# Routed experts computed only for their tokens, instead of every expert for every token

## The chip, the cores and the metric

The kernel runs on one core of one Trainium2 chip. The metric is the device time of one launch in microseconds, the median of three runs. The core has a matrix engine (TensorE, PE), a vector engine (VectorE, DVE), an activation engine (ScalarE, ACT), a general engine (GpSimd, POOL) and an engine that only issues transfers (SyncE, SP). Each works through its own list in order, and they wait for each other by semaphores.

## The reference

Four sublayers run one after the other on x of shape (2, 1024, 128), 2048 tokens, each as `x = x + layernorm(f(layernorm(x)))`: a 16-head attention, a mixture of experts, an 8-head differential attention, and a gated feed-forward. The change concerns the second:

```python
normed = h * rsqrt(mean(h*h) + 1e-8) * norm_weight
shared = relu(normed @ sw1 + sb1) @ sw2 + sb2            # 128 -> 512 -> 128
probs  = sigmoid(normed @ router_w.T)                    # 8 experts
scores, idx = top_k(probs, 2);  w = scores / (sum(scores) + 1e-6)
comb   = zeros(T, 8).at[arange(T)[:, None], idx].add(w)
eo     = relu(einsum('td,edh->teh', normed, ew1) + eb1) @ ew2 + eb2   # every expert, every token
out    = shared + einsum('teo,te->to', eo, comb)         # only 2 of 8 weights are not zero
```

## The kernel before, in words

Tokens lie in 16 tiles of 128, in four chunks of 512. All work is fp32; a product that goes through the fast fp32r mode is split into a high and a low part, three matmuls in place of one. The order on each engine is written out by hand, one function per stage and engine: `input_*`, `a0_*` (first attention), `f0_*` (mixture of experts), `a1_*` (second attention), `f1_*`. There is no planner; semaphore counts set what may overlap.

In `f0_pe` a chunk goes through nine experts, the shared one first. `up` is 4 hidden tiles by 3 matmuls of 128x512 (L999 to L1001); ACT applies bias and relu (L1081); `down` is 16 plain fp32 products of 128x128 (L1018; the trace shows two records for each); DVE multiplies by the routing weight and adds into Y (L1136). The shared result starts Y (L1092), and the biases of the second layer enter by a product with the transposed weights (`weights_turn` L1030, `bias` L1039). The routing runs on DVE in `f0_dve_route`, for eight tiles at a time: probabilities (L950, L951), best and second best (L953 to L959), weights (L961 to L967). Between experts of the first chunk the second to fourth chunk are normalised (`y0_norm`), transposed (`f0_pe_turn`, L390), split (`turn_act` L396, `turn_dve` L402) and given their logits (L928). The weight halves are made by ACT (L916) and POOL (L920). After each chunk DVE normalises it (`add_and_norm`); POOL supplies the reciprocal roots (`norm_rstd`, L313 and L316). During the last chunk, `a1_*_prepare` transposes the finished chunks and makes the first head's queries for the second attention. The last chunk is normalised in the first slots of that attention (`x1_stats`, and `x1_apply` on POOL).

Both attentions run in slots, one per 128 queries of a batch and head. In the first, SP copies queries and keys from one half of the partitions to the other (`a0_place_qk`, L823 to L831), two copies, a wait for them, and two more; the scores of a head wait for the last of these.

## Time and profile before

| what | value |
|---|---|
| median of 3 runs | 2020.68 us (2019.11 to 2021.67) |
| the profiled execution | 2021.03 us, its span 2019.2 us |
| PE busy | 1935.5 us, 96% of the span |
| DVE, ACT, POOL busy | 1512.6, 1384.8, 1123.5 us |
| mean granted clock of PE | 0.991 |

The span runs from the first to the last instruction. A share of busy time is a mean over all stages; the views of single stages say which engine sets the pace there. Start times of rows are microseconds from the start of the span.

### The profile page before, as it was taken

How to read it: one execution, taken by the hardware profiler on the slowest of the kernel's cores; microseconds unless marked ns; L12 is line 12 of the kernel's file. 1: busy time of each engine (PE TensorE's matmuls, PEld its weight loads, DVE VectorE, ACT ScalarE, POOL GpSimd, SP SyncE). 2: the span in 40 equal slices, each digit the busy share in tenths (PEclk: the TensorE clock that was granted, in tenths of full speed). 3: DMA queues.
4: the chain of work that ended last, by engine and by line, in shares of the span. 5: the costliest groups of instructions: out<-in, count | busy, mean ns of one | idle time of the engine just before them, and what ended most of it. 6: DMA issues, size and time to landing. Idle time of an engine off the chain costs nothing.

```text
span 2019.2 us, 37939 instructions
## 1 busy us (share of the span) xinstructions
PE 1935.5 (96%) x12066; PEld 1664.0 (82%) x12066; DVE 1512.6 (75%) x2595; ACT 1384.8 (69%) x2647; POOL 1123.5 (56%) x1364
## 2 busy tenths in 40 slices
PE   4999999999999999899999899999999999999788
PEld 3888888888888888689999688888888888888666
DVE  5988888888888888753223777777777777777775
ACT  3878787878787878544444677777777777777555
POOL 3655555555555555421000877777777777778522
PEclk9999999999999999999999999999999999999899
DMA  4212111111111111100000000000000000100000
GB/s 114 48 44 48 44 47 43 47 43 47 43 47 43 47 43 46 48 11 4 1 1 1 9 4 9 3 10 0 10 0 10 0 10 0 65 1 1 1 2 20
DMA packets 37767, 51.23 MB, mean 25 GB/s; under 512 B 8489, under 2 KB 17714, under 8 KB 37426
## 3 DMA queue, kind: packets, MB, share of 16 engines
q1 hardware_dynamic: 37682, 50.15, 9.8%
q8 instruction: 47, 0.77, 0.2%
q14 instruction: 38, 0.31, 0.1%
HBM read 15.52 MB, written 1.05 MB: 8 GB/s over the span
## 4 chain that ended last, share of the span: by engine, by line
PE 83%; DVE 6%; issue 4%; ACT 3%; POOL 2%; DMA 0%; SPq 0%; ACTq 0%; DVEq 0%; POOLq 0%
PE ps_t L546 7%; PE ps_o L556 7%; PE ps_t L1018 6%; PE ps_o L557 5%; PE ps_s L578 5%; PE ps_s L579 5%; PE ps_s L1436 5%; PE ps_s L1437 5%; PE ps_s L1438 5%; PE ps_t L1502 3%; PE ps_o L1518 3%; PE ps_o L1520 3%; PE ps_o L1519 3%; PE ps_s L999 2%; PE ps_s L1000 1%
## 5 line engine op out<-in xcount | busy, mean ns | idle before, releaser
L1649 DVE TENSOR_REDUCE a_negmax<-ps_s 128x1 f32<-128x1024 f32 x256 | 312.2, 1220 | 65.2 <-PE ps_s L1438 62.5
L720 DVE TENSOR_REDUCE a_negmax<-ps_s 128x1 f32<-128x1024 f32 x256 | 313.4, 1224 | 53.2 <-PE ps_s L579 38.2
L1573 ACT ACTIVATE a_p<-ps_s,a_negmax 128x1024 f32<-128x1024 f32 x256 | 286.5, 1119 | 93.6 <-DVE a_negmax L1649 92.2
L655 ACT ACTIVATE a_pth<-ps_t 128x512 fp32r<-128x512 f32 x512 | 278.6, 600 | 90.0 <-PE ps_t L546 89.9
L706 DVE TENSOR_TENSOR a_ptl<-ps_t,a_pth 128x512 fp32r<-128x512 f32 x512 | 327.5, 681 | 6.5 <-ACT a_pth L655 5.5
L783 POOL TENSOR_SCALAR a_p<-a_p,a_rsum 128x1024 f32<-128x1024 f32 x256 | 289.5, 1131 | 52.8 <-POOL a_rsum L779 52.8
L1744 POOL TENSOR_TENSOR a_p<-a_p 128x1024 f32<-128x1024 f32 x128 | 307.3, 2400 | 10.7
L779 POOL TENSOR_TENSOR a_rsum<-a_sum,minus_one 128x1 f32<-128x1 f32 x256 | 141.4, 552 | 307.5 <-ACT a_p L685 306.2
L685 ACT ACTIVATE a_p<-ps_s,a_negmax 128x1024 f32<-128x1024 f32 x256 | 288.7, 1128 | 15.3 <-DVE a_negmax L720 15.3
L546 PEld LDWEIGHTS ps_t<-ident_r,a_pr 128*128 128x128 f32 x2048 | 200.4, 140 | 32.0 <-POOL a_p L783 4.0
L556 PE MATMUL ps_o<-a_pth,a_v 128*128 128x512 f32 x512 | 219.9, 430 | 3.9 <-ACT a_o L664 1.3
L546 PE MATMUL ps_t<-ident_r,a_pr 128*128 128x128 f32 x2048 | 209.8, 245 | 3.5 <-DVE a_ptl L706 3.5
L578 PE MATMUL ps_s<-a_kh,a_q 128*128 128x512 f32 x512 | 202.0, 395 | 10.4 <-DMA a_kh<-a_kh 10.4
L1436 PE MATMUL ps_s<-xT_hi,a_q 128*128 128x512 f32 x512 | 203.4, 397 | 5.1 <-ACT a_p L1573 5.0
L1437 PE MATMUL ps_s<-xT_lo,a_q 128*128 128x512 f32 x512 | 203.1, 397 | 0.0
L1438 PE MATMUL ps_s<-xT_hi,a_q 128*128 128x512 f32 x512 | 202.8, 396 | 0.0
L579 PE MATMUL ps_s<-a_kl,a_q 128*128 128x512 f32 x512 | 202.0, 394 | 0.0
L1599 ACT ACTIVATE a_ath<-ps_t 128x512 fp32r<-128x512 f32 x256 | 139.2, 596 | 90.9 <-PE ps_t L1502 90.2
L557 PE MATMUL ps_o<-a_ptl,a_v 128*128 128x512 f32 x512 | 201.5, 394 | 0.0
L1683 DVE TENSOR_TENSOR a_atl<-ps_t,a_ath 128x512 fp32r<-128x512 f32 x256 | 163.6, 680 | 0.5 <-ACT a_ath L1599 0.5
L1081 ACT ACTIVATE f_h<-ps_s,f_b 128x512 f32<-128x512 f32 x144 | 97.8, 689 | 93.8 <-PE ps_s L1001 92.4
L313 POOL TENSOR_SCALAR rstd<-mv 128x4 f32<-128x4 f32 x28 | 6.9, 245 | 278.5 <-DVE mv L301 278.3
(251 smaller groups left out, 4527.3 us busy)
## 6 DMA issues: line engine op xcount, KB each, us to landing
a_q<-a_kh SPq DMA_DIRECT2D x64, 128.0 KB, 2.2
a_q<-a_kl SPq DMA_DIRECT2D x64, 128.0 KB, 2.3
a_kh<-a_kh SPq DMA_DIRECT2D x64, 128.0 KB, 2.2
a_kl<-a_kl SPq DMA_DIRECT2D x64, 128.0 KB, 2.3
a_w_raw<-in_l_w SPq DMA_DIRECT2D x8, 384.0 KB, 3.1
f_raw<-in_ffn_w SPq DMA_DIRECT2D x2, 1408.0 KB, 7.5
f_w_raw<-in_ffn_w SPq DMA_DIRECT2D x9, 256.0 KB, 4.7
f_w<-in_ffn_w SPq DMA_DIRECT2D x9, 256.0 KB, 4.5
```

The costliest lines, as they stand in the source:

```text
L546: ins = pe.transpose(ps_t[:, half, j * P:(j + 1) * P].bitcast(F32R), a0_pr[q % 4][:, k0:k0 + P], ident_r[:, :])
L556: pe.matmul(ps_o[:, :], a0_v[b][:, kt, j, :], a0_pth[par][:, kt, :], start=kt == 0, stop=False)
L557: ins = pe.matmul(ps_o[:, :], a0_v[b][:, kt, j, :], a0_ptl[par][:, kt, :], start=False, stop=kt == KT - 1)
L578: pe.matmul(ps_s[:, s % 2, half, :], queries, a0_kh[b][:, k], start=True, stop=False)
L579: ins = pe.matmul(ps_s[:, s % 2, half, :], queries, a0_kl[b][:, k], start=False, stop=True)
L706: dve.tensor_tensor(a0_ptl[(q // 4) % 2][at], ps_t[:, half, :].rearrange("p (t c) -> p t c", c=P), a0_pth[(q // 4) % 2][at], ALU.subtract) ...
L720: dve.tensor_reduce(a0_negmax[:, s % 4:s % 4 + 1], ps_s[:, s % 2, :, :], AX.XY, ALU.max, negate=True)\
L1436: pe.matmul(dst, a1_q[b][m][:, 0, qs], xT_hi[:, k], start=True, stop=False)
L1437: pe.matmul(dst, a1_q[b][m][:, 0, qs], xT_lo[:, k], start=False, stop=False)
L1438: ins = pe.matmul(dst, a1_q[b][m][:, 1, qs], xT_hi[:, k], start=False, stop=True)
L1649: dve.tensor_reduce(a1_negmax[:, s % 2, m:m + 1], ps_s[:, m, :, :], AX.XY, ALU.max, negate=True)\
L1744: pool.tensor_tensor(p1, p1, p2, ALU.add).then_inc(S["a1_combined"], 1)
```

## The change

The shared expert is still computed for all four chunks. The other eight are computed by blocks of 128 token-expert pairs. The tokens form two groups of 1024, with 2048 pairs each; each expert's pairs are rounded up to whole blocks, so a group takes at most 23 blocks, and always 23 are run, 46 in all.

- POOL makes constants at the start of the kernel, ahead of the first chunk's reciprocal root: 39 memsets, an `affine_select`, two iotas, and five copies or additions.
- During the second head of the first attention SP writes zeros and row numbers to two arrays in device memory, six DMAs with 128x23 pieces each: four with pieces of 256 bytes, two of 8 bytes.
- `f0_dve_route` now ends in sums over tiles, PE takes a prefix sum over partitions (`f0_pe_prefix`), and `f0_dve_place` (new, 13 dependent steps and three more instructions) makes from them each pair's row, and the list of experts of the blocks packed in three words a group. PE, ACT and DVE read six words into registers.
- POOL scatters each tile's rows (normed token, its number, its first expert) to device memory, twice, by indirect DMA: 16 per group. SP loads the sorted rows back in two DMAs a group.
- For each block: PE transposes the rows (four blocks in one bank), multiplies them with the expert's first layer (3 matmuls of 128x512, tokens as the stationary operand), DVE copies the result to SBUF, PE transposes it (4 of 128x128), ACT applies bias and relu (4 of 128x128), PE multiplies with the second layer (4 fp32 products of 128x128), DVE adds the bias, and POOL scatters the block's rows to their pairs' places by an indirect DMA.
- SP loads the two results of each token back, and DVE combines them by weight. For chunks 0 and 1 this, the normalisation and the preparation of the second attention run within the steps of the second group; for chunks 2 and 3 they run in slots 1 to 7 of the first head, whose other side work moves (the transposes of chunks 2 and 3 to slots 4 and 7).
- The transposes and biases by `weights_turn` and `bias`, `add_expert` and `add_and_norm` in this stage go.

The diff, cut to its core:

```diff
+    GROUPS = ((0, 1), (2, 3))
+    NB = (2 * GT * P + NR * (P - 1)) // P          # 23
+    ROUND = 4
+    BLOCKS = NG * NB                               # 46
+    SENT = 8
...
             pool.tensor_scalar(ident_r[:, :], ident[:, :], 1.0, 0.0, ALU.mult, ALU.add).then_inc(S["ident_ready"], 1)
+            f0_pool_const(pool)
             for c in range(NC):
                 norm_rstd(pool, NORM_IN + c, c)
...
                     a0_place_qk(sp, h * 4 + (len(A0_NEXT) + i), a0_splits(p, j, s, last), A0_PIECES[j][s])
+                    if isinstance(p, int) and p == 0 and j == 1 and i == 1:
+                        f0_clear_rows(sp)
...
+        def f0_clear_rows(sp):
+            sp.wait_ge(S["f0_const"], 2)
+            for g in range(NG):
+                rows = xs_dram[g].rearrange("(n p) d -> p n d", p=P)
+                sp.dma_start(rows[:, :, D:ROW], f0_tail[:, :, :]).then_inc(S["f0_zeroed"], 16)
+                for part in (slice(0, D // 2), slice(D // 2, D)):
+                    zero = f0_zero[:, :].rearrange("p (a d) -> p a d", a=1).broadcast_to([P, NB, D // 2])
+                    sp.dma_start(rows[:, :, part], zero).then_inc(S["f0_zeroed"], 16)
...
+        def f0_read_words(eng):
+            words = []
+            for g in range(NG):
+                eng.wait_ge(S["f0_words_ready"], g + 1)
+                for w in range(WORDS):
+                    words.append(eng.value_load(f0_words[0:1, g, w:w + 1], min_val=0, max_val=NR ** NR - 1))
...
+            def block_up(n, e):
+                r, cols = f0_round_of(n), f0_cols(n)
+                pe.wait_ge(S["f0_xs_lo_ready"], r + 1)
+                if n > 1:
+                    pe.wait_ge(S["f0_pre_ready"], n - 1)
+                bank = ps_s[:, 0, n % 2, :]
+                w_hi, w_lo = (w[:, bass.ds(e, 1), :].rearrange("p a n -> p (a n)") for w in (f0_w1_he, f0_w1_le))
+                pe.matmul(bank, f0_xs_hi[r % 2][:, cols], w_hi, start=True, stop=False)
+                pe.matmul(bank, f0_xs_hi[r % 2][:, cols], w_lo, start=False, stop=False)
+                pe.matmul(bank, f0_xs_lo[r % 2][:, cols], w_hi, start=False, stop=True).then_inc(S["f0_b_up"], 1)
+            def block_turn(n):
+                pe.wait_ge(S["f0_pre_ready"], n + 1)
+...
+            def block_down(n, e):
+                pe.wait_ge(S["f0_b_relued"], n + 1)
+                if n > 1:
+                    pe.wait_ge(S["f0_ys_ready"], n - 1)
+...
-                for pos in range(NE):
-                    up(pos)
...
-                    if pos:
-                        down(pos - 1)
...
+            up(0)
+            pe.wait_ge(S["a0_out_added"], 2 * H0)
+            f0_pe_logits(pe, 0)
+            down(0)
+            f0_pe_turn(pe, 1)
+            f0_pe_logits(pe, 1)
+            up(1)
+            down(1, lambda: route(0))
+            f0_pe_turn(pe, 2)
+            up(2)
+            pe.wait_ge(S["f0_prefix_out"], 1)
+            f0_pe_logits(pe, 2)
+            down(2)
+            f0_pe_turn(pe, 3)
+            f0_pe_logits(pe, 3)
+            up(3)
+            down(3, lambda: route(1))
+            expert = f0_read_words(pe)
+            turn_round(0)
+            for n in range(STEPS):
+                r = f0_round_at(n + 2)
+                if r is not None:
+                    turn_round(r)
+                if n < BLOCKS:
+                    block_up(n, expert(n))
+                if 1 <= n < BLOCKS + 1:
+                    block_turn(n - 1)
+                if n >= 2:
+                    block_down(n - 2, expert(n - 2))
+                a1_pe_prepare(pe, n)
...
+            def block_out(n):
+                e = expert(n)
+                dve.wait_ge(S["f0_b_down"], n + 1)
+                if n >= SENT:
+                    dve.wait_ge(S["f0_ys_sent"][n % SENT], 16 * (n // SENT))
...
+            def scatter(g, i):
+                if i == 0:
+                    pool.wait_ge(S["f0_pos_ready"], g + 1)
+                    pool.wait_ge(S["f0_zeroed"], 16 * 3 * NG)
+                for k in range(2):
+                    pool.indirect_dma_start(xs_dram[g][:, :], bass.IndirectOffsetOnAxis(ap=f0_pos[:, g, k, i:i + 1], axis=0),
+                                            f0_staged[c][:, i % TPC, :], None).then_inc(S["f0_scattered"][g], 16)
+            for i in range(GT):
+                scatter(0, i)
+                if i == 1:
+                    norm_rstd_rms(pool, norm_a0(2, 1), 2)
+                if i == 3:
+                    norm_rstd_rms(pool, norm_a0(3, 1), 3)
+            pool.wait_ge(S["f0_words_read"], 3)
+            for i in range(2):
+                scatter(1, i)
+            for n in range(BLOCKS):
+                if n % 2 == 0 and 2 + n // 2 < GT:
+                    scatter(1, 2 + n // 2)
+                send(n)
+                a1_pool_prepare(pool, n)
...
+        X1_SLOTS = {1: ((x1_combine, 2, 0), (x1_combine, 2, 1)), 2: ((x1_stats, 2, 0),), 3: ((x1_apply, 2, 0), (x1_stats, 2, 1)),
+                    4: ((x1_apply, 2, 1), (x1_combine, 3, 0), (x1_combine, 3, 1)), 5: ((x1_stats, 3, 0),),
+                    6: ((x1_apply, 3, 0), (x1_stats, 3, 1)), 7: ((x1_apply, 3, 1),)}
```

## Rows read from the trace of the kernel before

**Rows 1.** Busy time in stretches: PE, weight loads, DVE, ACT, POOL; clock; DMA; GB/s.
```profile
851.60:1107.90 256.30, 248.54 (x1716) 226.36 (x1714) 88.29 (x336) 115.12 (x178) 29.11 (x37) 0.99 0.03 10
937.87:996.79 58.92, 58.92 (x411) 53.82 (x409) 17.28 (x69) 25.34 (x39) 6.60 (x10) 1.00 0.00 1
1107.90:1160.80 52.90, 45.35 (x237) 35.82 (x236) 39.70 (x74) 31.02 (x59) 41.33 (x38) 0.94 0.03 8
1209.50:1307.50 98.00, 97.53 (x607) 83.65 (x606) 77.10 (x132) 70.79 (x149) 74.00 (x86) 1.00 0.02 7
```

**Rows 2.** The chain that ended last, 800 to 1160 us: start, us, what.
```profile
800.93 0.64 PE ps_t L546 x8
...
937.87 0.44 PE ps_o L1030 x4
938.31 3.57 PE ps_t L1018 x32
941.88 1.08 PE ps_o L1039 x8
```

**Rows 3.** Groups of instructions by shape, 800 to 1160 us: busy us, mean ns, idle before.
```profile
L1081 ACT ACTIVATE f_h<-ps_s,f_b 128x512 f32<-128x512 f32 x144 | 97.8, 689 | 93.8 <-PE ps_s L1001 92.4
...
L1136 DVE SCALAR_TENSOR_TENSOR Y<-ps_t,f_comb,Y 128x128 f32 x64 | 18.1, 345 | 66.2 <-PE ps_t L1018 65.9 <-DVE Y L1127 0.2
...
L1744 POOL TENSOR_TENSOR a_p<-a_p 128x1024 f32<-128x1024 f32 x7 | 16.7, 2383 | 0.6
...
L316 POOL TENSOR_TENSOR rstd<-rstd,minus_half 128x4 f32<-128x4 f32 x12 | 12.5, 1040 | 2.2 <-POOL rstd L313 2.2
```

**Rows 4.** Timeline, 838 to 885 us: second chunk and first routing (start, us, engine).
```profile
859.42 0.72 PEld L390 LDWEIGHTS ps_t<-ident,xst 128*128 128x128 f32 x4 [4.07 <-DVE xst L307]
...
861.19 0.63 PE L1001 MATMUL ps_s<-xT_hi,f_w_lo 128*128 128x512 f32 x1
...
861.87 0.69 DVE L402 TENSOR_TENSOR xT_lo<-f_nT,xT_hi 128x512 fp32r<-128x512 f32 x1 [2.51 <-ACT xT_hi L396]
...
865.50 0.21 ACT L935 ACTIVATE f_prob<-ps_m 128x64 f32<-128x64 f32 x1
865.67 1.26 POOL L920 TENSOR_TENSOR f_w_lo<-f_w_raw,f_w_hi 128x512 fp32r<-128x512 f32 x1 [1.87 <-ACT f_w_hi L916]
865.74 1.24 DVE L950 TENSOR_SCALAR f_tmp<-f_prob 128x64 f32<-128x64 f32 x1 [3.17 <-ACT f_prob L935]
867.02 0.55 DVE L951 RECIPROCAL f_prob<-f_tmp 128x64 f32<-128x64 f32 x1
...
868.12 0.23 DVE L955 TENSOR_TENSOR f_tmp<-f_tmp,f_rank 128x64 f32<-128x64 f32 x1
```

**Rows 5.** DVE's timeline, 926 to 938 us: second routing, first step.
```profile
927.03 0.18 DVE L950 TENSOR_SCALAR f_tmp<-f_prob 128x64 f32<-128x64 f32 x1
```

**Rows 6.** Timeline, 885 to 945 us: SP issues a transfer.
```profile
904.45 0.33 SPq L1803 DMA_DIRECT2D a_w_raw<-in_l_w  x1
```

**Rows 7.** Timeline, 0 to 62 us: the kernel's start.
```profile
0.28 0.10 POOL L2125 MEMSET const-float32-1.0<- 128x1 f32 x1
...
5.24 0.23 POOL L313 TENSOR_SCALAR rstd<-mv 128x4 f32<-128x4 f32 x1 [2.97 <-DVE mv L301]
```

**Rows 8.** Line 1662 by itself: register instructions of DVE's queue.
```profile
L1662 DVEq FUSED_REGOPS  x12: 46/52/64, 1209.2 to 1700.7; - x12
```

**Rows 9.** SP's timeline, 60 to 150 us.
```profile
93.25 0.58 SPq L831 DMA_DIRECT2D a_kl<-a_kl  x1
108.51 0.46 SPq L823 DMA_DIRECT2D a_q<-a_kh  x1
```

**Rows 10.** DMA, whole span: the kernel's own queue.
```profile
q1 hardware_dynamic: 37682, 50.15, 9.8%
```

**Rows 11.** DMA, 2013 to 2019.2 us: the last stores.
```profile
DMA packets 1057, 0.53 MB, mean 86 GB/s; under 512 B 32, under 2 KB 1056, under 8 KB 1056
...
out<-X SPq DMA_DIRECT2D x2, 256.0 KB, 2.5
```

More of the change, by code:

```diff
@@ new lines, in f0_sp, with f0_round_at, f0_round_of @@
+            load(0)
+            load(1)
+            for c in range(2):
+                got(c)
+            a1_load_next(sp, 0, True)
+            for c in range(2, NC):
+                got(c)
+        STEPS = BLOCKS + 2
+        def f0_round_at(block):
+            g, j = divmod(block, NB)
+            if block < BLOCKS and j % ROUND == 0:
+                return g * len(ROUNDS) + j // ROUND
+            return None
+        def f0_round_of(block):
+            g, j = divmod(block, NB)
+            return g * len(ROUNDS) + j // ROUND
```

944 lines of the change are left out of this document (574 added, 370 removed), and 4 rows, old and new, of the table A1_SPARE.

## The prediction

> **What bounds the kernel now.** The table of before is read first: PE is busy for 96% of the span, DVE for 75%, so the first question of a change is how much of PE's work it takes away, and the second which engine then sets the pace. The busy times in stretches say where the changed stage lies: from the first product of the shared expert at 851.6 us to the first scores of the second attention at 1107.9 us, 256.3 us, in which PE is busy for 248.5, DVE for 88, ACT for 115 and POOL for 29 [rows 1]. A chunk in steady state takes 58.92 us of unbroken PE work [rows 1]. In the chain the second layer of an expert is 3.57 us, and what is no expert's is 0.44 and 1.08 us of routing transposes and biases [rows 2]; so an expert is (58.92 - 1.52) / 9 = 6.38 us, its first layer 2.81 us, or 0.234 us for each of 12 matmuls. In the groups by shape ACT (L1081) and DVE (L1136) stand idle before their instructions for more or nearly as long as they work, both on PE [rows 3]. The stage is PE's alone.
>
> **The sum is made against** the profiled execution: span 2019.2 us, time 2021.0, so 1.8 us lie around the span; the median of the runs is 0.3 us under that time.
>
> **Start of the kernel.** POOL's constants stand ahead of the first reciprocal root, which began at 5.24 us [rows 7]. 39 memsets at 0.10 us [rows 7] are 3.9 us, eight other short ones at about 0.25 us (as L313, rows 7) 2 us, and five waits of some 0.2 us 1 us: 7 us from 2.3 us on. The root starts at 9.3 us at most, 4 us late; memsets overlap in part, and nothing else hides it, since all of the attention waits for it. I take 3 us; ends 0 (full overlap) and 10 us (an iota at the longest POOL row, 2.4 us [rows 3], each).
>
> **Clearing the rows.** 128 x 23 pieces x 6 DMAs are 17,664 packets, 1104 for each of 16 DMA engines. The last stores move 1057 packets, most of 512 bytes, in about 1.7 us at 9 tenths, some 28 ns per packet and engine (256 KB each land 2.5 us after issue) [rows 11]. The mean over the queue is 0.098 x 16 x 2019.2 / 37682 = 84 ns, with larger packets [rows 10]. At 28 ns the clear holds the queue for 31 us. SP issues it behind the copy at 93.25 us, and its next copy is due at 108.51 [rows 9]: that one lands behind the clear at about 127 us in place of 111. Three more dependent rounds of some 3 us bring the last to 136 us; the next head is due some 10 us before that. I take 10 us, by the row nearest in size. Ends: 0 (packets that cost by their bytes, 14 ns) and 72 us (84 ns, a queue held until 187 us).
>
> **From the first shared product to the first block.** As before, the second chunk's transposes can start at 859.4 and its low half is ready at 862.6 [rows 4], since DVE's chain ahead of them is unchanged; PE fills that time with the first chunk's second layer. Routing of a group is 13 small DVE steps of 0.26 us with the gap (0.23 busy, L955), a reciprocal of 0.55, four sums: 5.1 us. Placement is 13 more steps and three instructions: 3.6 us. Group 0: 862.6 + 5.1 = 867.7, prefix product 0.5, placement to 872. The third chunk's two norms are 7 us on DVE and POOL, so its transposes come at 879, its low half at 882; 7.3 us of PE (6.38 and the logits) and 2.9 us for the next turn give 892.5; route, prefix and placement 9.2 us: 901.7. Reading six words has no row; I take 3 us, from a bound of six register instructions (0.05 us each [rows 8]) to six transfers in a row (2.5 us each, rows 11: 15 us). Transposing and splitting the first rows: 2 us. The matmul of 0.63 us instead of 0.39 after a 4 us gap shows PE at half clock there, 1.2 GHz [rows 4]; four such gaps cost 1 us each. First block at 907 + 4 = 911 us. ACT's and POOL's weight halves lie in PE's gaps.
>
> **An indirect DMA.** The trace has none. POOL writes out 128 rows each time. Below it lies SP's issue of a plain one, 0.33 us [rows 6]; above it POOL's longest instruction, 2.4 us (L1744); nearest is POOL's power of 4 elements a partition, 1.04 us (L316) [rows 3], work done by a routine. With one issue on top I take 1.4 us. Group 0's 16 scatters and two roots (2.8 us) run from 872 to 897, land at 900, and are read back by 903: just ahead of the first block.
>
> The Trainium skill, page "DMA: Bandwidth & Descriptors", section "Latency and other measured facts", puts the first byte of a POOL-issued DMA at about 1 us for writing its descriptors. By that price the sum below would be the same, since POOL would be 30 us further from being the bound.
>
> **The blocks.** PE, per block: first layer 3 x 0.234 = 0.70; four transposes at 0.08 (eight in 0.64 [rows 2]) 0.32; second layer 4 x 3.57 / 16 = 0.89; the rows' own transpose 0.08: 1.99 us. ACT: four relus of 128 columns, at most 0.3 us each (0.21 for 64 columns [rows 4], 0.69 for 512 [rows 3]): 1.2. DVE: a copy of 512 columns, 0.69 as L402 [rows 4], and 0.35 for the bias add as L1136 [rows 3], a quarter of 0.69 for the split: 1.2. Neither is the bound, and with two buffers each has a step of slack. POOL: 62 indirect DMAs x 1.4 = 87 us, and 10 us of roots and key splits: 97 us over the loop. PE: 46 x 1.99 = 91.5, preparation of the second attention 5.5, two steps to fill and drain 4, register arithmetic of 0.05 us twice per step [rows 8] 4.6: 106 us. So the loop ends at 1017, against 1107.9: a gain of 91 us. In it DVE also has 9 us per finished chunk (8 weighted adds, two norms) spread over 23 steps with 0.9 us free in each. The wait of `block_out` for an eighth send back has behind it DVE's copies, and so PE; POOL falls 10 us behind by block 10 (4 + 12 + 11 DMAs are 38 us, the steps 24) and is level by block 30, inside its eight buffers.
>
> **The first head.** Before, its first 52.9 us held 45.4 us of PE at clock 0.94 and 39.7 of DVE [rows 1]: it already waited for the last chunk's norms. Later a head is 98 us with DVE at 77 [rows 1], 4.8 of 6.1 us per slot. Now two chunks (18 us of DVE) come in slots 1 to 7, where before there were about 5, with POOL's part moved to DVE; and slot 1 waits for the last block's rows, which need a send, 2.5 us to land, and a load of 2.5. 13 us more of DVE against 13 us free, and 5 us of waiting at a point that also waited before: 8 us, ends 0 and 20. DVE's score maxima queue behind that wait, and PE behind them.
>
> **Sum:** 3 + 10 - 91 + 8 = -70; 2019.2 - 70 + 1.8 = **1951 us**.
>
> **The rivals.**
> *POOL sets the loop's pace.* In POOL's list all 78 DMAs follow one another from 872 us with 18.5 us of other work and waits. The stage's end is 890.5 + 78 d. For d = 1.4 that is 1000, under PE's 1017; from d = 1.6 POOL decides. What would bring it there: blocked access. When POOL's subtraction of 1.26 us ran beside DVE's `tensor_scalar` from SBUF to SBUF, that took 1.24 us [rows 4] in place of 0.18 [rows 5]; the two exclude each other. If DVE's copies (0.69 us a step) shut POOL out likewise, d is 2.1: end at 1054, gain 54, time 2021.0 - 54 + 21 = 1988 us. Against: the copy reads PSUM. The skill's page "SBUF — State Buffer", section "SBUF: two separate sides", warns that a POOL-issued DMA waits for a two-port copy on DVE and advises issue from SP; by its rule, which is for SBUF to SBUF, only the norms' instructions would block, and d stays near 1.5.
> *Slower: the price of an indirect DMA.* The same formula, with rows written out one by one in software at 3 us: end at 1124.5, a loss of 17 and the 21 of the other terms: 2059 us. The point from which it decides is 890.5 + 78 d = 1087, d = 2.5 us, just over POOL's longest row. For it: no row is of this kind; against: 128 small entries are less work than that row's 1024 columns.
> *The clear holds up the first attention* at 84 ns a packet: 62 us more, 2013 us. Against: its packets are smaller than the mean's.
> *PE's clock falls in the loop.* PE waits every step for DVE and ACT; at half clock the matmul rows show 0.63 for 0.39 and steps would be some 3.5 us: 70 us more, 2021 us. Against: PE is busy 1.99 of some 2.2 us, and clock 0.94 was kept at 45.4 of 52.9 us busy [rows 1].
> That the saving is not there cannot be: 46 blocks are run in place of 128 products of a tile with an expert, whatever the routing.
>
> **How the numbers follow.** Forecast 0.60; POOL's pace 0.17; slower by the DMA's price 0.10; the clear 0.08; the clock 0.05. A measurement of this kernel tells 0.2%, 4 us. Slower by more: 0.10 and a third of the last two: 0.14; within: 0.03; faster: 0.83. The range leaves out the slow rival and little below: low end, start, clear and head at 0 and POOL cheap, 1951 - 21 - 12 for the words and gaps = 1918; high end, past POOL's pace, the clear and the clock: 2025. The forecast alone would have 1920 to 1985.
>
> **What would show it.** In the profile after: first block matmul near 911 us plus what the start adds; 46 blocks at 2.1 to 2.3 us, PE over 85% busy in them at clock 1.00; POOL's indirect DMAs at 1.4 us, and DVE's Y or PE waiting for none of them; first scores of the second attention near 1030 us; a stall of PE of some 10 us near 130 us, released by the copies of keys. Wrong would be a loop in which PE waits on DVE behind POOL's DMAs, a stall of tens of us in the third head of the first attention, or a granted clock near 0.5 in the loop.

## The result and the profile after

The changed kernel takes 1993.4 us (median of 4 runs, 1990.0 to 1998.8) against 2020.5 us of the kernel before in the same comparison (4 runs, 2019.1 to 2021.7): ratio 0.987, 95% interval 0.984 to 0.990. It is faster, by 27 us (1.3%) where 70 were forecast. 1993 lies inside the range of 1918 to 2025; the point is 42 us off. The profiled execution took 1990.0 us with a span of 1988.2, so 31.0 us of span are to be explained.

The busy times in stretches, after, are cut at the same events as [rows 1] (columns: us, then PE, weight loads, DVE, ACT, POOL with instruction counts, granted clock, DMA share, GB/s): first shared product to the first scores of the second attention; the first and the second half of the loop over blocks; first scores to the first maximum of slot 8.

```profile
875.40:1056.50 181.10, 146.02 (x1000) 126.97 (x998) 114.04 (x343) 82.91 (x237) 101.79 (x110) 0.92 0.22 69
942.70:992.30 49.60, 48.69 (x349) 42.91 (x349) 24.44 (x52) 28.24 (x94) 30.50 (x32) 0.95 0.24 76
992.30:1056.50 64.20, 56.83 (x417) 49.18 (x417) 45.35 (x133) 35.11 (x113) 34.48 (x38) 1.00 0.16 52
1056.50:1130.40 73.90, 47.76 (x235) 38.63 (x235) 58.90 (x120) 30.61 (x59) 35.89 (x33) 0.84 0.06 17
```

The whole span then falls into four terms, each by two events that both profiles have:

| from the profiles, us | before | after | difference | forecast |
|---|---|---|---|---|
| first scores of the first attention | 31.3 | 33.0 | +1.8 | +3 |
| first shared product, less the line above | 820.4 | 842.4 | +22.0 | +10 |
| to the first scores of the second attention | 256.3 | 181.1 | -75.2 | -91 |
| from there to the end of the span | 911.4 | 931.8 | +20.4 | +8 |
| sum | 2019.2 | 1988.2 | -31.0 | -70 |

The saving is there: PE, busy for 248.5 us of the stage before [rows 1], is busy for 146.0. What the forecast lacks is 12 us in the clear, 8 us each in the prologue (first shared product to first block) and in the loop over blocks, which the third line holds together, and 12 us in the first head; the start came 1 us cheaper than forecast.

**The clear.** (The six DMAs that write zeros and row numbers.) PE's waits between 60 and 160 us (line, releaser, us in total, times, longest):

```profile
PE ps_s L643 <- DMA a_kl<-a_kl: 19.8, 1, 19.8
```

and the DMA view from 95 to 140 us (busy tenths of the queues in 40 slices, then packets, then the kernel's own queue):

```profile
DMA  8789999999999999999999999999999999982007
...
DMA packets 18191, 3.81 MB, mean 85 GB/s; under 512 B 17840, under 2 KB 17840, under 8 KB 18187
...
q1 hardware_dynamic: 18187, 3.77, 130.1%
```

The share passes 100% because packets overlap. The queues are full until about 136 us, and SP itself stands at its issues (its timeline; a plain issue is 0.6 us):

```profile
95.11 0.60 SPq L1142 DMA_DIRECT2D f_xs_rows<-f_tail  x1
95.74 7.08 SPq L1145 DMA_DIRECT2D f_xs_rows<-f_zero  x2
```
```profile
110.56 12.34 SPq L1145 DMA_DIRECT2D f_xs_rows<-f_zero  x2
122.94 8.35 SPq L888 DMA_DIRECT2D a_q<-a_kh  x1
```

This is the shape that was foretold (a stall near 130 us, released by the copies of keys), but 20 us long and with PE at the lower clock behind it (granted 0.50 from 130 to 140 us and 0.53 in the next 10).

**The prologue.** First shared product 875.4, first block 942.7 us: 67.3 us, forecast 59.4. DVE's and POOL's timelines in the first routing, and DVE's in the second (start, us, engine, line, shapes, idle before):

```profile
887.80 1.00 DVE L1022 TENSOR_TENSOR f_one<-f_tmp,f_idx 128x64 f32<-128x64 f32 x1
888.83 1.21 DVE L1024 SCALAR_TENSOR_TENSOR f_left<-f_one,f_prob 128x64 f32<-128x64 f32 x1
...
892.80 0.94 DVE L1022 TENSOR_TENSOR f_one<-f_tmp,f_idx 128x64 f32<-128x64 f32 x1
```
```profile
887.43 8.66 POOL L986 TENSOR_TENSOR f_w_lo<-f_w_raw,f_w_hi 128x512 fp32r<-128x512 f32 x7
```
```profile
927.00 0.22 DVE L1022 TENSOR_TENSOR f_one<-f_tmp,f_idx 128x64 f32<-128x64 f32 x1
927.26 0.22 DVE L1024 SCALAR_TENSOR_TENSOR f_left<-f_one,f_prob 128x64 f32<-128x64 f32 x1
...
928.54 0.23 DVE L1022 TENSOR_TENSOR f_one<-f_tmp,f_idx 128x64 f32<-128x64 f32 x1
```

The same instructions take 0.94 to 1.21 us beside POOL's seven weight halves and 0.22 without them: the first routing took 10.7 us, the second 5. (Both operands of these instructions lie in SBUF, the memory the engines work in; tiles named ps_ are PE's results in another memory, PSUM.)

**The loop.** First block to first scores 113.8 us, forecast 106. Groups of instructions on POOL between 900 and 1060 us, and PE's waits in the loop's second half:

```profile
L1484 POOL DMA_INDIRECT f_ys_rows<-f_ys,f_dst x46 | 45.0, 978 | 42.9 <-DVE f_ys L1406 37.6 <-issue 5.3
L1475 POOL DMA_INDIRECT f_xs_rows<-f_staged,f_pos x32 | 32.0, 1000 | 25.5 <-DVEq L1212 12.3 <-issue 8.9 <-DVE f_pos L1061 4.2
```
```profile
PE ps_s L1282 <- DVE f_pre L1399: 6.4, 6, 1.5
```

An indirect DMA is 0.98 us on POOL, 1.26 with the issue behind it, and POOL is idle for 43 us beside its 46 sends: it sets no pace. PE's granted clock is 0.95 in the loop's first half, its start included, and 1.00 in the second.

**The first head.** From the first maximum of the scores to the first one of slot 8 it is 49.9 us before and 72.3 after. DVE's and POOL's timelines of two stretches in it, and PE's longest idle time:

```profile
1064.07 4.71 DVE L1757 SCALAR_TENSOR_TENSOR Y<-f_got,f_top,Y 128x128 f32<-128x128 f32 x8
...
1078.44 3.19 DVE L371 TENSOR_SCALAR xhat<-Y,mv,rstd 128x128 f32<-128x128 f32 x4
...
1087.97 3.13 DVE L371 TENSOR_SCALAR Y<-X,mv,rstd 128x128 f32<-128x128 f32 x4
```
```profile
1064.44 2.37 POOL L2105 TENSOR_TENSOR a_p<-a_p 128x1024 f32<-128x1024 f32 x1
...
1078.81 2.48 POOL L2105 TENSOR_TENSOR a_p<-a_p 128x1024 f32<-128x1024 f32 x1
...
1088.34 2.43 POOL L2105 TENSOR_TENSOR a_p<-a_p 128x1024 f32<-128x1024 f32 x1
```
```profile
1091.21 1.09 PE L454 MATMUL ps_t<-ident,Y 128*128 128x128 f32 x4 [9.74 <-issue]
```

The two groups of norm applications (L371) end when POOL's long addition does: 1081.63 and 1081.29, 1091.10 and 1090.77 us. The combination (L1757) ends 2 us behind it, and takes 2.4 us when nothing is in its way. PE, whose turn of chunk 2's rows stands in its order between two sets of scores, stood 9.7 us for the second group. In the loop the same four applications took 1.1 us. The granted clock of this stretch is 0.84, where the first head before had 0.94 [rows 1].

### The profile page after: what moved, and what is told of

The parts are those of the page before. It is cut to its first block, busy times and chain, and to the rows that moved or that the text cites. A ratio compares the mean times of both kernels' runs of the same rounds, so it can differ in the third digit from the quotient of the medians.

```text
span 1988.2 us, 37557 instructions
## 1 busy us (share of the span) xinstructions
PE 1838.5 (92%) x11354; PEld 1569.9 (79%) x11354; DVE 1558.7 (78%) x2650; ACT 1351.4 (68%) x2707; POOL 1195.9 (60%) x1481
## 4 chain that ended last, share of the span: by engine, by line
PE 41%; DVE 7%; issue 4%; ACT 2%; POOL 1%; DVEq 0%; ACTq 0%; POOLq 0%
PE ps_s L1804 5%; PE ps_s L1803 5%; PE ps_s L1805 5%; PE ps_t L1861 3%; PE ps_o L1877 3%; PE ps_o L1879 3%; PE ps_o L1878 3%; PE ps_t L1290 2%; DVE a_negmax L2007 2%; PE ps_m L1898 1%; PE ps_t L1585 1%; PE ps_s L2239 1%; PE ps_s L2240 1%; PE ps_m L1900 1%; PE ps_m L1899 1%
## 5 line engine op out<-in xcount | busy, mean ns | idle before, releaser
L2105 POOL TENSOR_TENSOR a_p<-a_p 128x1024 f32<-128x1024 f32 x128 | 307.4, 2401 | 10.7
L1959 ACT ACTIVATE a_ath<-ps_t 128x512 fp32r<-128x512 f32 x256 | 139.2, 596 | 99.2 <-PE ps_t L1861 98.4
L2099 POOL TENSOR_SCALAR a_p<-a_p,a_c 128x1024 f32<-128x1024 f32 x128 | 144.4, 1128 | 21.9 <-DVE a_c L2020 20.0
L1877 PE MATMUL ps_o<-a_ath,a_xh 128*128 128x256 f32 x512 | 148.2, 289 | 0.6 <-DVE a_atl L2043 0.6
```

The costliest lines, as they stand in the source:

```text
L2105: pool.tensor_tensor(p1, p1, p2, ALU.add).then_inc(S["a1_combined"], 1)
```

## The experiments

Two theories stood against each other: that each of the four terms is its own wait, above all DVE's instructions between SBUF and SBUF standing still while POOL works (theory), and that these are amounts of work or packets that no order changes (rival). 15 runs, of 13 kernels, were made in four comparisons, each beside the kernel before on one chip; two kernels ran twice. Times are medians; "stage" times are from the profiles.

### The clear

`spread_clear` issues the six DMAs at four places of the first pair; `tails_apart` moves two of them.

```diff
-                    if isinstance(p, int) and p == 0 and j == 1 and i == 1:
-                        f0_clear_rows(sp)
+                    if isinstance(p, int) and p == 0 and (j, i) in {(0, 1): (0, 1), (0, 3): (2,), (1, 1): (3, 4), (1, 3): (5,)}:
+                        f0_clear_rows(sp, ...)          # spread_clear: which of the six DMAs
+                    ... in {(0, 1): (0, 3), (1, 1): (1, 2, 4, 5)}:   # tails_apart
```

> The six clearing DMAs of the row scratch are issued at four places of the first head pair (two, one, two, one) instead of all six at one. Nothing is left out. Theory (the clear costs by the length of its one burst: 17,664 packets held the queue about 43 us and the pieces of the keys behind it came late, PE idle 19.8 us at L643; the gap that such a transfer may fill without harm is about 20 us): bursts of 14 and 7 us are both under it, the idle of 19.8 us and the half clock behind it go, time 1993 - 21 = about 1972 us, first shared product near 854 us instead of 875. Rival A (the cost is the total of packets, wherever they stand): four smaller stalls with the same sum, about 1993 us. Rival B (what the attention before loses is taken up by later slack): under 5 us of change.

> The two DMAs of 8-byte tails (5,888 packets, 2% of the bytes) go at the first place of the first head, the four DMAs of 256-byte zeros (11,776 packets, 98% of the bytes) stay where all six were. Nothing is left out. Theory (packets set the length of a burst, about 38 ns times one sixteenth each): the burst that is left takes 28 us of which about 20 are free, so 8 us of stall are left of 22: about 1979 us. Rival (bytes set it): the burst keeps 98% of its length, about 1993 us. Rival C (8-byte writes are the dear ones, several times the price of a 256-byte one): the stall goes altogether here, about 1972 us, or moves to the first head, about 1993 us with the idle time at the tails.

`spread_clear`: 1970.8 us, ratio to before 0.976 (0.974 to 0.977); first shared product at 853.1 us. No wait of PE for copies is left in this stretch (one of 10.4 us at the start of the attention is there in the kernel before too), and its clock is whole (120 to 140 us, where the kernel after has PE busy for 5.58 us at clock 0.72):

```profile
120.00:140.00 20.00, 20.00 (x132) 17.43 (x131) 16.96 (x22) 15.34 (x30) 9.42 (x12) 1.00 0.59 82
```

So the clear costs nothing once it is dealt out (853.1 us is the 851.6 of before and the 1.8 of the start), and the changed kernel lost 22.3 us: 21.3 of them up to its last scores, by its one burst, and 1.0 by a clock that fell ahead of the first shared product (see `early_norms`). Rivals A and B fall. `tails_apart`: 1989.4 us (0.983, 0.981 to 0.985), first shared product at 870.4 us; the stall is shorter, by less than the count of packets says:

```profile
PE ps_s L643 <- DMA a_kl<-a_kl: 11.9, 1, 11.9
```

The last scores of the first attention start at 829.4 us with the clear spread, 844.0 here and 850.7 in the kernel after: 14.6 and 21.3 us of loss for 11,776 and 17,664 packets. The traces give the prices directly. In `tails_apart` the four DMAs of zeros run alone (its DMA view from 96 to 131 us):

```profile
DMA  9799999999999999999999999999999999996000
```

These 11,776 packets of 256 bytes took 32 us, 43 ns for each on its one of 16 engines. In `spread_clear` a DMA of 8-byte packets ran nearly by itself, and the view from 97.2 to 99.2 us has

```profile
DMA packets 3168, 0.08 MB, mean 39 GB/s; under 512 B 3167, under 2 KB 3167, under 8 KB 3168
```

which is 10 ns each. So neither packets alone nor bytes alone set the length. The burst of 32 us lost 14.6 us and the one of 40 us lost 21.3, so some 18 us of a burst cost nothing here, an estimate from these two runs.

### The prologue

`halves_on_dve` gives DVE the seven subtractions:

```diff
             y0_norm(dve, 4, 3)
+            for pos in range(2, NE):
+                f0_pool_w1_lo(dve, pos)
             f0_dve_turn(dve, 3)
...
-            for pos in range(2, NE):
-                f0_pool_w1_lo(pool, pos)
```

> The seven subtractions that split the routed first-layer weights (L986, 1.0 to 1.2 us each on POOL between 887 and 896 us) are issued by DVE in its idle time before the third chunk's shared product is added, and no longer by POOL. Nothing is left out. Theory (DVE instructions with both inputs in SBUF wait while POOL works on SBUF; in the routing of the first group they took 0.94 to 1.2 us where the same ones took 0.22 in the second): the first routing falls from 10.7 to 5 to 6 us, the scatters start some 4 to 5 us earlier, and the first block starts 2 to 5 us earlier, if nothing else holds it: about 1989 us. Rival (those long times are DVE's own, through waits on the semaphores of the steps): the routing stays at 10.7 us, the added 3 to 5 us of subtractions come on top, 1993 to 1997 us.

1993.9 us (0.986, 0.984 to 0.988), not to be told from the kernel after. In its profile the first shared product comes 3.6 us later, in code that the edit doesn't touch: the clear stalled PE 1.1 us longer, and the rest is waiting and lower clock around it. The routing itself went as the theory said, 889.7 to 894.3 us, and the seven halves took 4.29 us of DVE's idle time:

```profile
891.49 0.23 DVE L1022 TENSOR_TENSOR f_one<-f_tmp,f_idx 128x64 f32<-128x64 f32 x1
891.75 0.22 DVE L1024 SCALAR_TENSOR_TENSOR f_left<-f_one,f_prob 128x64 f32<-128x64 f32 x1
...
893.03 0.22 DVE L1022 TENSOR_TENSOR f_one<-f_tmp,f_idx 128x64 f32<-128x64 f32 x1
```
```profile
908.25 1.12 PE L454 MATMUL ps_o<-ident,f_staged 128*128 128x128 f32 x4 [8.89 <-DVE f_staged L371]
```

The first block started 63.9 us after the first shared product (67.3 in the kernel after). Of the 6 us that the routing gained, DVE then waited 2.1 for PE's prefix product, so that the scatters began 4 us sooner after the first shared product; the way goes on through PE's wait of 8.9 us for chunk 2's norm, which DVE did behind the placement and POOL's root behind four scatters. `early_norms` takes that order apart, on top of `spread_clear`:

```diff
+            for stage in range(1, 4):
+                y0_norm(dve, stage, 2)
             f0_dve_route(dve, 0)
-            y0_norm(dve, 1, 2)
+            y0_norm(dve, 4, 2)
             f0_dve_place(dve, 0)
...
+            norm_rstd_rms(pool, norm_a0(2, 1), 2)
             for i in range(GT):
                 scatter(0, i)
-                if i == 1:
-                    norm_rstd_rms(pool, norm_a0(2, 1), 2)
```

> Built on the spread clear. DVE does chunk 2's norm ahead of the first routing and its last step ahead of the placement, chunk 3's right behind it, the seven weight halves are DVE's, POOL's root for chunk 2 stands ahead of the scatters, and PE runs the first prefix behind the second chunk's shared product. Nothing is left out. Theory (the way to the first block runs through chunk 2's and 3's norms, their turns and the second routing, not through the first group's scatters, which are done 10 us early; PE stood 8.9 us at L454 for chunk 2): PE's turn of chunk 2 comes 8 to 9 us earlier, the first block 6 to 10 us after the first shared product sooner (58 to 61 us instead of 67.4): 8 us less than spread_again. Rival (the scatters and the load of the first group's rows end last once they start later): 0 to 3 us.

First block 61.5 us after the first shared product, against 67.3 in `spread_again` beside it: 5.8 us, a little under what was expected. The total is 1967.2 us (0.973, 0.972 to 0.975) against 1969.7, only 2.5 us less, though the profiled executions differ by 7.3 (that of `spread_again` was its slowest run). The profile of `spread_clear`, the same program as `spread_again`, is near its median and shows where the rest can go. Its span is 2.5 us longer too: the prologue gives 5.9, but ahead of the first shared product 2.1 us are lost, in code that is the same in both, and 1.7 behind the first scores of the second attention. PE's last stretch of the first attention, in `spread_clear` and in `early_norms` (busy times as above):

```profile
828.42:854.14 25.72, 20.29 (x128) 16.38 (x127) 17.38 (x43) 11.14 (x22) 11.63 (x14) 1.00 0.15 51
```
```profile
827.94:856.16 28.22, 23.05 (x127) 19.10 (x126) 16.92 (x43) 11.09 (x20) 11.65 (x14) 0.88 0.19 59
```

The same products keep PE busy for 2.8 us more at clock 0.88. PE idles for 1.9 and 2.0 us in this stretch in both, and behind these gaps its matmuls of 512 columns stand at 0.63 us in place of 0.39 in `spread_again`, `early_norms` and `all_changes`, and not in `spread_clear`, `even_steps` and `head_order`. Why one profiled execution has it and another not is open. So a difference of 2 to 3 us between two profiles needs a look at this stretch first. The first placement now ends at 879 us with the scatters behind it, so the way through the norms and the second routing was the longer one.

### The first head

`x1_light` leaves out three quarters of chunk 2's and 3's work in the slots.

```diff
-            for i in range(TPC):
+            for i in range(TPC if c < 2 else 1):
```

> In the first head's slots of the second attention the weighing of the sent results, the two applications of the norm and the addition between them handle one tile of four for chunks 2 and 3 (for chunks 0 and 1 all of them): three quarters of that work is left out. Theory (these DVE instructions between SBUF and SBUF wait for POOL's long ones: 956 and 836 ns each where the same took 341 to 369 ns in the loop): 24 applications at 0.9 us, 12 weighings at 0.5 us and three quarters of two additions go, 25 to 29 us of DVE time of which most stood on the path, and the first head gets 15 to 20 us shorter (73.9 to about 56 us from first scores to the eighth slot): about 1976 us. Rival (it is the plain amount of work, at the loop's times of 0.35 and 0.25 us): 7 to 10 us shorter, about 1985 us. Rival 2 (the head waits for the fetched results or for PE's order of turns, not for DVE): under 3 us.

1983.1 us (0.980, 0.978 to 0.982). From the first to the last scores of the second attention it is 11.7 us shorter than in the kernel after, and slot 8 comes at 60.3 us instead of 72.3: between the two theories. What stays shows why. The addition, now of one tile of 128x128, waited for POOL all the same:

```profile
1080.60 2.38 DVE L1778 TENSOR_TENSOR X<-X,xhat 128x128 f32<-128x128 f32 x1
```

So the wait doesn't shrink with the work, and this run could not part the theories. `short_pool` leaves DVE's work whole and takes POOL's away, on top of `spread_clear`:

```diff
-                p2 = a1_p[a1_tile_of(s, 1) % 4][1][:, :]
+                p2 = a1_p[a1_tile_of(s, 1) % 4][1][:, 0:8 if isinstance(h, int) and h == 0 and s <= 8 else SEQ]
```

> Built on the spread clear (1970.8 us). In the first eight slots of the first head of the second attention POOL's two long instructions (scaling the second softmax and adding it to the first, 1.12 and 2.4 us over 1024 columns) work on 8 columns of 1024: the rest of that work is left out. DVE's work is untouched. Theory (the first head is long because DVE's instructions between SBUF and SBUF stand while POOL's long ones run): the groups of four applications fall from 3.1 to 4.0 us to about 1.4, the first eight weighings from 4.7 to about 2.1, together 10 us off DVE's path, and the eighth slot starts at 60 to 64 us after the first scores instead of 72.3 to 73.5: total 1958 to 1963 us. Rival (the amount of DVE's work and the order of the slots are what costs, POOL only stands beside it): no more than 3 us, 1968 us or above.

Slot 8 came at 60.3 us after the first maximum, against 73.5 in `spread_clear`, and first to last scores are 13.4 us shorter: the theory's number. DVE's groups are at their plain length:

```profile
1060.83 2.42 DVE L1760 SCALAR_TENSOR_TENSOR Y<-f_got,f_top,Y 128x128 f32<-128x128 f32 x8
...
1072.59 1.11 DVE L371 TENSOR_SCALAR xhat<-Y,mv,rstd 128x128 f32<-128x128 f32 x4
...
1080.04 1.10 DVE L371 TENSOR_SCALAR Y<-X,mv,rstd 128x128 f32<-128x128 f32 x4
```

The total, 1974.8 us (0.977, 0.976 to 0.979), shows none of it, because in this comparison the loop took 126.5 us instead of 113.8 and the prologue 71.9 instead of 67.4, both in code that the edit doesn't touch; that is taken up below. The 17.2 us lost there and the 13.4 won make the 4 us by which it is slower than `spread_clear`. `apply_on_act` moves the applications to ACT, and `head_order` also puts the turns at slots 5 and 7:

```diff
+            for t in range(TPC):
...
+                ins = act.activation(dst, src, ACT.Identity, bias=nmr[:, k, t:t + 1], scale=rstd[:, x1_par(c, i), t:t + 1])
...
-            {0: ("m",), 1: ("wt", 0), 2: ("wt", 1), 4: ("turn", 2), 5: ("q", 1, 0), 6: ("q", 1, 1), 7: ("turn", 3),
+            {0: ("m",), 1: ("wt", 0), 2: ("wt", 1), 5: ("turn", 2), 6: ("q", 1, 0), 7: ("turn", 3), 8: ("q", 1, 1),
```

> Built on the spread clear (1970.8 us). In the first head's slots the four applications of the norm for chunks 2 and 3 (16 instructions of 128x128) go from DVE to ACT, as Identity with a scale and a bias per row, the bias made by two small POOL instructions; the addition and the second statistics come at the end of the slot, and the two turns of rows stand behind the weighing of the keys on PE and behind the first softmax on ACT. Nothing is left out. Theory (13.4 us of DVE time in this stretch are these applications, 8 of them waiting for POOL, and PE stands 9.7 and 4.4 us at L454 behind them): the eighth slot starts about 60 us after the first scores instead of 73.5: total 1956 to 1961 us. Rival (ACT becomes late instead: 16 instructions at 0.25 to 0.3 us are 4 to 5 us on an engine that has them free, but each sits ahead of a softmax): 1966 to 1975 us.

1981.8 us (0.980, 0.978 to 0.982), again with the long loop (127.9 us) and prologue (73.1 us). Slot 8 at 63.5 us, 10 sooner; what is missing to 60 is a wait that the edit itself made, ACT's for the root, with a softmax behind it:

```profile
1087.78 1.65 ACT L1806 ACTIVATE Y<-X,xst,rstd 128x128 f32<-128x128 f32 x4 [4.68 <-POOL xst L1818]
```

> Built on the spread clear. As apply_on_act (the applications of the norm for chunks 2 and 3 on ACT in the first head), and the turns of their rows stand at slots 5 and 7, chunk 3's combination and statistics a slot earlier. Nothing is left out. Theory (in apply_on_act ACT stood 4.7 us for the root at slot 4 with a softmax behind it, PE 5.5 us at its turn; all else was as long as a plain head): the eighth slot starts 60 to 62 us after the first scores, against 73.5 with the spread clear alone and 66.8 in apply_on_act: 11 to 13 us less than spread_again. Rival (the waits for POOL only move to the combinations, which stay on DVE): 7 us less, no better than apply_on_act's head.

1958.4 us (0.969, 0.967 to 0.970) against 1969.7 of `spread_again` beside it: 11.3 us less, slot 8 at 60.9 us: the theory's numbers, with nothing left out. The combinations stayed on DVE and still took 4.7 and 5.0 us, and PE stood 3.8 us behind the second, so this head is not free of the wait.

### The loop and the words

`even_steps` changes at which steps the second attention's preparation stands; `fixed_experts` leaves out the words and the choice of the expert.

```diff
-        A1_APPLY = {NB + 7: (0, 0), NB + 10: (0, 1), NB + 15: (1, 0), NB + 18: (1, 1)}
-        A1_TURNS = (NB + 12, NB + 20)
+        A1_APPLY = {NB + 7: (0, 0), NB + 11: (0, 1), NB + 17: (1, 0), NB + 21: (1, 1)}
+        A1_ADD = {NB + 8: 0, NB + 18: 1}
+        A1_TURNS = (NB + 12, NB + 22)
...
-                return (words[g * WORDS + j // NR] >> (3 * (j % NR))) & (NR - 1)
+                return j * NR // NB
```

> Built on the spread clear (1970.8 us). The second attention's preparation inside the loop over blocks is dealt out so that no step has both an application and an addition, or a combination and a turn: DVE's extra work in a step is at most 1.8 us instead of 2.1 to 2.9. Nothing is left out. Theory (in the second half of the loop PE waited 6.4 us for DVE's copies of the first layer, because a step with 3.3 us of DVE work is longer than PE's 2.16): the loop from the first block to the second attention's first scores falls from 113.7 to 109 to 111 us, total 1966 to 1968 us. Rival (the sum of DVE's work in the second half, 38 us of 50, is what counts, or PE's own instructions for the preparation): within 1.5 us of 1970.8.

> Built on the spread clear (1970.8 us). No engine reads the packed words, and the expert of a block is a constant of the program: left out is the choice of the expert from the data, so the blocks are computed with a given one. Everything else is as it was. Theory (reading six words costs DVE and PE 3.9 to 4.1 us ahead of the first block, and the register arithmetic in a step is mostly hidden: PE's steps are 1.96 us of matmuls with 0.3 to 0.4 us of issue in every second): the first block starts about 4 us earlier, the loop gets 2 to 7 us shorter (46 steps at 1.96 to 2.1 instead of 2.15): total 1960 to 1965 us. Rival (the gaps of 0.3 to 0.4 us are fetches of instructions, not registers, and the reading lies beside other work): within 2 us of 1970.8.

By their totals (1987.0 and 1979.0 us; 0.983, 0.982 to 0.985, and 0.979, 0.978 to 0.981) both are slower than `spread_clear`, which says nothing of the edits: the loops of all four kernels of this comparison were 9 to 14 us longer than 113.8, most of it (10 to 12 us) between steps 7 and 16. Their prologues were disturbed too: in each of them ACT stood 7.5 to 7.9 us ahead of a copy of a chunk's norm for a releaser that the profile doesn't know, and in the three that read the words the first block came 71.9 to 73.1 us after the first shared product instead of 67.4. Read by steps, `even_steps` took 35.3 us for its last 14 steps instead of 41.1, and gave 3.5 back between the last block and the first scores, where its last turn and queries had come to stand: 2.4 us, under what was expected. Of `fixed_experts` the prologue can be read beside the three others: 68.4 us, so 3.5 to 4.7 us less without the words, as the theory had it. What it won in the loop could not be read.

> The kernel of spread_clear once more, unchanged, so that what is run beside it can be compared on one chip. Theory (in short_pool, apply_on_act, fixed_experts and even_steps the loop's steps 7 to 16 took 10 to 13 us longer than in all runs before, with ACT and DVE standing together, in code that two of them don't touch: it depends on the chip or the day, not on these edits): on the chip of those four it takes 1983 to 1988 us, on the other 1971 us. Rival (their edits or their place in memory did it): 1971 us everywhere.

1969.7 us (0.974, 0.973 to 0.976), on the chip of the four, with a loop of 113.7 us: the chip did not make the long loops. That the edits didn't either is shown further down, by one program that ran both ways. The parts were then put together:

> Spread clear, early norms, the head's order, and the dealt-out steps of the loop with the last turn and queries one step earlier. Nothing is left out. Theory (the places are apart and each wait is its own): the sum, 8 + 12 + 3 = 23 us less than spread_again, 1948 us on the chip without the stall in the loop. Rival (what one place gives, the next takes, since the second attention's preparation waits for what is sent back): 12 us or less.

1952.2 us (0.966, 0.964 to 0.967), 17.5 us less than `spread_again`; 23 were expected. Against the profile of `spread_clear` its prologue is 5.9 us shorter (8 expected), its loop 3.3 (3 expected) and what follows the first scores 11.2 (12 expected), and 1.8 us are lost by the clock ahead of the first shared product. It is 41 us under the changed kernel's time, though the two were not run beside each other.

> The kernel of all_changes once more, as the measure for the two beside it: 1950 to 1954 us if nothing disturbs the loop.

1965.5 us (0.973, 0.971 to 0.975): the program of `all_changes`, 13.3 us slower, with nearly all of the difference in the loop (first block to first scores 123.4 us against 110.5). So the long loop comes without any edit, and on both chips. In its steps 7 to 16 ACT and DVE stood together and went on in the same instant:

```profile
946.00 0.29 DVE L1411 TENSOR_TENSOR f_ys<-ps_t,f_b 128x128 f32<-128x128 f32 x1 [6.11 <-remote]
```
```profile
946.00 1.14 ACT L1356 ACTIVATE f_bh<-ps_s,f_b 128x128 f32<-128x128 f32 x4 [4.64 <-remote]
```

The releaser is none that the profile knows; POOL's indirect DMAs stay at 0.96 us. In `late_reading`, whose code is laid out otherwise, the long steps are others. That it is the fetching of instructions would fit both, but no run tells it, and why one comparison has it and another not stays open. The changed kernel itself was profiled without it.

`late_reading` puts the reading of the words behind the first round's turn and split, `late_fixed` leaves the words out on top of that:

```diff
-            expert = f0_read_words(pe)
             turn_round(0)
+            expert = f0_read_words(pe)
```

> Built on all_changes. PE turns the first round of rows, ACT copies it and DVE takes the rest ahead of their reading of the packed words instead of behind it, the weights of the two choices are worked out at steps 8 and 12 of the loop, and POOL's root for chunk 3 stands behind four scatters instead of eight. Nothing is left out. Theory (PE's reading of six words, 4.1 us, stands alone on the way to the first block, and DVE's chain of 3.8 us of reading and 3.2 us of weights behind it; the root for chunk 3 was 4.8 us late): first block 6 to 9 us sooner than in all_again (61.4 us after the first shared product), total 6 to 9 us less. Rival (the load of the first group's rows or the weight halves end last then): 2 to 4 us less.

> The kernel of late_reading with the expert of each block a constant of the program: left out are the reading of the words and the choice of the expert from the data. Theory (reading costs 3.9 us of PE even where the rows' turn stands ahead of it, of which the split of the round, 3 us, hides most; register arithmetic costs 0.35 us of issue in every fourth step, 4 us over the loop): 4 to 6 us less than late_reading. Rival (registers are free, the gaps are the fetching of instructions): within 1.5 us of late_reading.

`late_reading`: 1962.8 us (0.972, 0.970 to 0.973), 2.7 less than `all_again`: the rival's number. Its first block comes 58.0 us after the first shared product, against 62.6, so 4.6 of the expected 6 to 9 us, and the loop, disturbed in both, is no measure for the rest. `late_fixed`: 1953.1 us (0.967, 0.965 to 0.968). Its first block comes 2.0 us sooner still, and its last 28 steps take 65.7 us. That is 2.8 us less than in `late_reading`, of which two steps are disturbed even there (2.6 and 2.9 us where `all_changes` has 1.9 and 2.4), and 2.0 less than in `all_changes`: 0.07 to 0.10 us a step. So registers cost some 3 to 5 us over 46 steps, an estimate from these 28, and the 4 of the theory and the 4.6 of the forecast lie in it. The rest of the 9.7 us is in the disturbed steps and not explained, so the total, well over the theory's 4 to 6 us, proves nothing.

## Why the prediction was off

**Right.** The direction and its reason (PE's work goes, and the loop is PE's: busy for 48.7 of 49.6 us in its first half); the start (+1.8 us, 3 forecast); the split of an indirect DMA's price on POOL, 1.26 us with its issue against 1.4, so the rival *POOL sets the loop's pace* and the one on the slower side, which needed 2.5 us, did not come; a granted clock near 1 in the loop (0.95 and 1.00 in its halves); the register arithmetic, as far as the runs can tell. The place of the clear's stall was right too. That 1993 lies in the range is luck in part: the range was spanned by the rivals, POOL's pace at 1988 among them, and none of these came; four terms of the forecast were each too small instead.

**"I take 10 us"** for the clear, from 28 ns a packet. The burst held the queues for 40 us, not 31, some 18 us of it cost nothing, not 21, and the loss was 21 us, by `spread_clear`. The mechanism was as told and the term mis-sized: the row at hand was of 512-byte stores at the end, and a packet of 256 bytes here cost 43 ns, more than that row and not less. Why is not shown; the two differ also in that all zeros are read from one tile. (The 28 ns themselves are right, the words for them are not: 1.7 us at 9 tenths would be 23 ns, while the view's busy share, 29.8% of 6.2 us, gives 28.) The upper end of the term (72 us) had room for it; the value was chosen too near the lower.

**"First block at 911 us"**, 59.4 us after the first shared product; it took 67.3. Two steps failed. "Routing of a group is 13 small DVE steps of 0.26 us" left out what else ran then: "ACT's and POOL's weight halves lie in PE's gaps" is true of PE and false of DVE, whose steps with two operands in SBUF took up to 1.2 us beside them; `halves_on_dve` took 6 us out of the routing and 3.4 out of the prologue by moving them. And "its transposes come at 879" had the third chunk's norm beside the routing, where the code puts it behind the placement and its root behind scatters; `early_norms` shows that order to be worth 5.8 us together with the halves. Reading the words was 4.1 us on PE and 3.8 on DVE, 3 forecast.

**"106 us"** for the loop, 113.8 measured. 46 blocks at 1.99 us with registers come to 2.09 a step, and the first half ran at 2.15. The rest is "spread over 23 steps with 0.9 us free in each": an even spread, where the code puts a norm's application and its addition, or a combination and a turn, into one step, some 3 us of DVE for 2.15 of PE. PE waited 6.4 us for DVE's copies in the second half; `even_steps` shortened those steps by 5.8 us and lost part of it at the loop's end.

**"8 us"** for the first head; it was 20.4. "13 us more of DVE against 13 us free" counted the work at its plain length. The prediction itself had the row that speaks against this, POOL's and DVE's instructions excluding each other [rows 4, 5], and used it for the rival on the indirect DMAs alone, where it did not matter. In this head POOL works 3.5 us in each slot, and DVE's groups between SBUF and SBUF waited 2.0 to 2.9 us each. `short_pool` takes 13.4 us back by POOL's work alone, `head_order` 11.3 with nothing left out.

Four costs were taken at their lower or plain size, and that is one error made four times. The rival *clear at 84 ns* was right in kind, since the clear did hold up the first attention, though by 21 us and not by 72: its chance of 0.08 should have raised the forecast's own term.

The Trainium skill, page "SBUF — State Buffer", section "SBUF: two separate sides", gives the rule behind the misses in the prologue and in the first head: DVE and GpSimd share a port pair that one of them holds for a whole instruction. The traces agree (0.22 against 0.94 to 1.2 us, 1.1 against 3.1 to 4.0 us). Its warning on DMAs that POOL issues speaks of a DVE copy in a two-port mode; here the same was seen beside subtractions with both operands in SBUF: while DVE did the seven halves in `all_changes` one indirect DMA took 4.58 us instead of 0.96.

```profile
890.80 4.30 DVE L987 TENSOR_TENSOR f_w_lo<-f_w_raw,f_w_hi 128x512 fp32r<-128x512 f32 x7
```
```profile
891.35 4.58 POOL L1480 DMA_INDIRECT f_xs_rows<-f_staged,f_pos  x1 [0.30 <-issue]
```

## What to carry to other kernels

Before an engine's free time is counted as room for moved work, look at what the other side of a shared port does in that time: DVE's work between SBUF and SBUF beside long POOL instructions costs what is left of POOL's instruction and not its own length. `head_order` moved it to ACT. DVE's maxima over PSUM stayed at 1.22 us beside POOL, so operands in PSUM may serve as well, which no run tried. A transfer in thousands of small pieces is dealt out in bursts shorter than the slack of what queues behind it; here six DMAs at one place cost 21 us and at four places nothing. And extra work in a pipelined loop is summed per step, not per loop: the longest step counts.

## What the runs showed of the hardware

- An indirect DMA of 128 rows from POOL takes 0.98 us of POOL in the mean of 46 and 1.00 in that of 32 (0.96 in most), with 0.30 us to the next, and lands 2.3 us after issue (median, 2.2 at least), for rows of 520 and of 512 bytes alike.
- Writes from SBUF in a long burst cost 43 ns per packet of 256 bytes on one of the 16 DMA engines, and 10 ns per packet of 8 bytes (`tails_apart`, `spread_clear`). A burst also holds SP at its issues: 7.1 to 12.3 us for one or two DMAs in place of 0.6 each.
- DVE and POOL exclude each other in both directions: 3.1 to 4.0 us for four DVE instructions that take 1.1 alone, 4.58 us for an indirect DMA of 0.96.
- One and the same program took 1952.2 us in one comparison and 1965.5 in another, with 12 us more in ten fixed steps of unrolled code, while the kernel before stayed within 0.1%.
- Behind two gaps of 1.9 and 2.0 us PE's granted clock fell in some profiled executions and not in others of the same code (mean 0.88 against 1.00 over some 26 us), which cost 2.8 us.
